# A linear-attention stage between two expert blocks on one core: float32 key sums, scanned value sums, a softmax centred by ScalarE's bias, a state masked by GpSimd, and a new order of the stages

## The chip, the cores and the metric

The kernel runs on one core of one Trainium2 chip. Its engines are called PE (TensorE, matrix products; PEld is its weight load), DVE (VectorE), ACT (ScalarE), POOL (GpSimd) and SP (SyncE, which issues DMAs here). The metric is device time in microseconds (us) from launch to end, the median of several runs. Matrix products write to PSUM, eight banks of 128 x 512 float32; all else lies in SBUF. POOL works on SBUF alone here.

## The reference

One sequence of T = 2048 tokens with 128 features goes through three residual blocks, each behind a layer norm: an expert feed-forward (one shared and eight routed experts, the best two per token), an attention with 64 slots per head, and the same feed-forward again. The attention, for each of four heads of 32 features:

```
wk = exp(clip(x @ sk_w1 @ sk_w2 + sk_b2)); zk = cumsum(wk, over time)
S = where(mask, q @ k.T, 0)
p = softmax(S @ wk * scale / zk)                  # over 64 slots
wv = exp(clip(x @ sv_w1 @ sv_w2 + sv_b2)); zv = cumsum(wv, over time)
A = where(mask, (p / zv) @ wv.T, 0)
o = A @ v;  o = rmsnorm(o) * gnorm_w * g * sigmoid(g);  out = o @ Wo
```

So two running sums over time are wanted (zk and zv, 256 columns each for the four heads), and their inverses, and two products with a causal mask.

## The kernel before

Tokens are cut into 16 chunks of 128 (chunk c, its parity p for double buffers, its place n in the loop). What lies before a chunk is kept in PSUM as a running state: `state_ps` holds K'wk (256 columns) and wv'v (128 columns), and only the blocks in which both sides belong to one head are wanted. `copy_state` on ACT copies just these blocks to `state`, in six instructions, into a tile whose other parts were set to zero once.

A chunk passes through four stages, one step of the loop each; in one step the engines work at four chunks, called front, mid, last and end. There are 19 steps: four written out, twelve in a hardware loop of two steps a turn, three to drain. Each engine has its own list of what it does in a step, in a fixed order (`attn_step`), and waits on semaphores; the order written there is the order in which it runs.

Before the change, front projects q, k (`project`) and the slot logits (`slot_logits`), applies the rotary embedding (DVE multiplies, `rope_multiply`; POOL adds, `rope_add`), splits q and k into float16 parts (`qk_high`, `qk_low`), turns them (`turn_qk`), and multiplies and masks S (`scores`, `mask_s`). It clips and exponentiates the slots (`clip_slots`, `slots_exponent`), 512 columns for keys and values together, and splits the result into three bf16 parts: `slots_high` on ACT, `slots_rest` on POOL, `slots_middle` on ACT, `slots_low` on POOL. Mid sums the parts over time with a triangle of ones, three products of 512 columns (`running_sums`), and later adds the rest of the chunk in the same way (`add_sums`), so that `sum_ps` carries the sum on. The sum is inverted by a logarithm, an exponential and one Newton step (`sums_log`, `sums_first_inverse`, then on DVE `sums_product` and `sums_inverse`). Mid also turns the value slots (`turn_v`, `copy_value_slots`), forms the logits from the state and the chunk, scales them, takes the smallest per head (`soft_min`), subtracts it (`soft_centre`), exponentiates (`soft_exp`), multiplies by the inverse value sum (`prob_scale`) and turns the product (`turn_p`, `copy_p`). Last forms A (`weights_a`, `mask_a`) and o (`outputs`), divides by the softmax sum (`norm_shares`), gates (`gate_o` on POOL), and prepares the root mean square (`o_square`, `norm_squares`, `norm_variance`; `root_o` on POOL raises to the power -1/2). End applies it (`norm_apply`), turns, projects (`turn_o`, `copy_o`, `out_proj`) and adds the result to x (`add_y`).

While the loop drains, the next block's layer norm begins. In the step of the last chunk's outputs, DVE takes the moments of the first twelve chunks (`early_moments`), after `mask_a` and before `norm_shares`. POOL takes two roots from them in `tokens(2, 0, 2)`, called ahead of its list for that step; DVE uses them in two calls of `centre` ahead of the next step. Lines named below by L and a number are those of the profile.

## Time and profile before

| what | value |
|---|---|
| median of 3 runs | 506.77 us (506.55 to 506.98) |
| the profiled execution's own time, and its span | 506.91 us, 504.9 us |
| busy: PE, DVE, ACT, POOL | 446.7, 433.5, 316.5, 166.0 us |
| mean granted TensorE clock | 0.97 of full |

A busy share is an average over stages, and PE's busy time counts matrix products whose ends are modelled. Start times are from the start of the span. The attention stage fills about 192 to 345 us.

### The profile page before, as it was taken

Reading aid. Unit: us, or ns where it says so; the run is one execution under the profiler, and the core shown is the slowest. Engines: PE = TensorE matmul, PEld = TensorE weight load, DVE = VectorE, ACT = ScalarE, POOL = GpSimd, SP = SyncE. Lnnn points to the kernel's source line nnn. Section 1 sums busy time; section 2 is a strip of 40 time slices with the busy share of each in tenths; the row PEclk is TensorE's granted clock in tenths of the full one; section 3 lists DMA queues with packets and bytes.
Section 4 is the critical chain, followed back from the end, with each engine's and each line's share of the span. In section 5 each row is a group of like instructions: output and inputs, shape, how many; then the busy total and the mean of one; then the engine's idle time right before and its main releaser. Section 6 shows DMA issues by size and latency. Waiting matters only on the chain.

```text
span 504.9 us, 12339 instructions
## 1 busy us (share of the span) xinstructions
PE 446.7 (88%) x3879; PEld 313.0 (62%) x3895; DVE 433.5 (86%) x1139; ACT 316.5 (63%) x683; POOL 166.0 (33%) x199
## 2 busy tenths in 40 slices
PE   0787899999999775999999999975899999999996
PEld 0444566666666463788888888764456666666664
DVE  3699999999999963799999999975899999999996
ACT  3544455555555476889898989845555555555553
POOL 2999990000000236466666666633000000000000
PEclk9999999999999987799999999995999999999999
DMA  6222000000000000000000000000000000000002
GB/s 214 87 70 81 1 1 0 0 0 0 0 0 1 1 2 0 2 0 1 1 1 0 0 0 0 0 1 1 1 1 2 0 0 0 0 0 0 0 0 83
DMA packets 6697, 6.98 MB, mean 14 GB/s; under 512 B 818, under 2 KB 5170, under 8 KB 6676
## 3 DMA queue, kind: packets, MB, share of 16 engines
q1 hardware_dynamic: 6532, 6.33, 4.2%
q10 hardware_dynamic: 144, 0.39, 0.2%
q8 instruction: 11, 0.18, 0.2%
q14 instruction: 10, 0.08, 0.1%
HBM read 5.67 MB, written 1.05 MB: 13 GB/s over the span
## 4 chain that ended last, share of the span: by engine, by line
PE 55%; DVE 20%; ACT 10%; issue 8%; POOL 4%; DMA 1%; DVEq 1%; POOLq 0%; ACTq 0%
PE bank L1131 16%; PE bank L1143 10%; PE bank L1145 10%; PE bank L1144 10%; DVE h L807 4%; DVE h_lo L813 2%; ACT gate_s L313 2%; ACT qk_t L382 2%; DVE x L796 2%; DVE stats L705 1%; DVE pz L937 1%; PE bank L1325 1%; POOL rstd L543 1%; ACT slot_b L362 1%; ACT h_hi L318 1%
## 5 line engine op out<-in xcount | busy, mean ns | idle before, releaser
L318 ACT ACTIVATE h_hi<-h 128x512 f16<-128x512 f32 x144 | 90.7, 630 | 133.0 <-DVE h L807 133.0
L807 DVE SCALAR_TENSOR_TENSOR h<-bank,gate_s 128x512 f32<-128x512 f32 x144 | 99.4, 690 | 25.5 <-ACT gate_s L313 19.7
L1131 PE MATMUL bank<-w_hi,h_hi 128*128 (+1 forms) x576 | 104.9, 219 | 15.1 <-DVE h_lo L813 10.4
L1143 PE MATMUL bank<-xt_hi,w_hi 128*128 128x512 f16 x288 | 110.6, 384 | 0.0
L1144 PE MATMUL bank<-xt_hi,w_lo 128*128 128x512 f16 x288 | 110.4, 383 | 0.0
L1145 PE MATMUL bank<-xt_lo,w_hi 128*128 128x512 f16 x288 | 110.2, 383 | 0.0
L1131 PE MATMUL bank<-w_hi,h_lo 128*128 (+1 forms) x576 | 104.4, 219 | 0.0
L1131 PE MATMUL bank<-w_lo,h_hi 128*128 (+1 forms) x576 | 104.4, 219 | 0.0
L813 DVE TENSOR_TENSOR h_lo<-h,h_hi 128x512 f16<-128x512 f32 x144 | 102.4, 711 | 0.1
L796 DVE SCALAR_TENSOR_TENSOR x<-bank,wts,x 128x128 f32<-128x128 f32 x288 | 86.5, 343 | 1.3 <-PE bank L1131 0.9
L313 ACT ACTIVATE gate_s<-bank 128x512 f32<-128x512 f32 x144 | 83.4, 579 | 0.0
L1131 PEld LDWEIGHTS bank<-w_hi,h_hi 128*128 128x128 f16 x576 | 56.1, 97 | 39.9 <-DVE h_lo L813 13.1
L1131 PEld LDWEIGHTS bank<-w_lo,h_hi 128*128 128x128 f16 x576 | 56.3, 98 | 12.0
L1131 PEld LDWEIGHTS bank<-w_hi,h_lo 128*128 128x128 f16 x576 | 56.3, 98 | 0.0
L1145 PEld LDWEIGHTS bank<-xt_lo,w_hi 128*128 (+1 forms) x288 | 28.5, 99 | 34.8 <-issue 1.7
L541 POOL TENSOR_SCALAR var_e<-mv 128x4 f32<-128x4 f32 x12 | 3.4, 283 | 114.1 <-issue 93.7
L1143 PEld LDWEIGHTS bank<-xt_hi,w_hi 128*128 (+1 forms) x288 | 28.4, 99 | 19.3 <-issue 1.3
L1144 PEld LDWEIGHTS bank<-xt_hi,w_lo 128*128 (+1 forms) x288 | 28.4, 99 | 18.1 <-issue 1.1
L1098 PE MATMUL bank<-cst,xn 128*128 128x128 f32 x48 | 11.5, 392 | 14.6 <-ACT xn L290 14.6
L290 ACT ACTIVATE xn<-x,shift,rstd 128x128 f32<-128x128 f32 x32 | 13.6, 483 | 14.1 <-DVE shift L716 13.8
L620 POOL TENSOR_TENSOR slot_r<-slots,slot_b 128x512 f32<-128x512 f32 x16 | 18.5, 1158 | 8.9 <-ACT slot_b L362 5.9
L625 POOL TENSOR_TENSOR slot_b<-slot_r,slot_b 128x512 bf16<-128x512 f32 x16 | 18.4, 1153 | 3.5 <-ACT slot_b L367 3.5
(160 smaller groups left out, 851.7 us busy)
## 6 DMA issues: line engine op xcount, KB each, us to landing
wf<-in_w_ffn SPq DMA_DIRECT2D x8, 384.0 KB, 3.1
...
```

Source lines behind the costliest of these rows:

```text
L290: i = act.activation(xn[:, g % 2, c, :], x[:, g * GT + c, :], ACT.Identity, bias=shift[:, g, c:c + 1], scale=rstd[:, g, c:c + 1])
L313: act.activation(gate_s[:, ih, :], gate_ps[ih][:, :], ACT.Silu, scale=1.0 / (XS * WS)).then_inc(silu_done, 1)
L318: act.activation(h_hi[:, g, ih, :], h32[:, ih, :], ACT.Copy).then_inc(hhi_done, 1)
L620: nc.gpsimd.tensor_tensor(slot_r[:, :], slots[:, p, :], slot_b1[:, p, :], ALU.subtract).then_inc(S["slots_rest"], 1)
L625: nc.gpsimd.tensor_tensor(slot_b3[:, p, :], slot_r[:, :], slot_b2[:, p, :], ALU.subtract).then_inc(S["slots_b3"], 1)
L796: i = nc.vector.scalar_tensor_tensor(x[:, t, :], down_ps[j][:, c % 2 * P:(c % 2 + 1) * P], wts[:, t, e:e + 1] if isinstance(e, int) else w ...
L807: nc.vector.scalar_tensor_tensor(h32[:, ih, :], up_ps[ih][:, :], HS / (XS * WS), gate_s[:, ih, :], ALU.mult, ALU.mult).then_inc(hmul_done, 1)
L813: nc.vector.tensor_tensor(h_lo[:, g, ih, :], h32[:, ih, :], h_hi[:, g, ih, :], ALU.subtract).then_inc(hlo_done, 1)
L1131: i = mm(dst, hp[:, g, ih, c * P:(c + 1) * P], wcols(wp, e, at, D), start=(k == 0), stop=(k == 3 * IH - 1))
L1143: mm(ps[:, :], wcols(w_hi, e, at, P), xt_hi[:, ts], start=True, stop=False)
L1144: mm(ps[:, :], wcols(w_lo, e, at, P), xt_hi[:, ts], start=False, stop=False)
L1145: mm(ps[:, :], wcols(w_hi, e, at, P), xt_lo[:, ts], start=False, stop=True).then_inc(done, 1)
```

## The change

The three bf16 parts are dropped. Key sums are one float32 product of 256 columns with the triangle (and one with its rest), straight from `slots`. Value sums are taken on DVE: `turn_v` moves to the front stage, where the slots lie turned with time along the columns, and `value_sums` runs a scan over the 128 columns of each half, which starts from the last column of the chunk before. The inverse is formed as before, in two halves where its input comes from two places. The softmax is no longer centred by DVE: `soft_exp` passes the smallest value as the bias of four instructions, one a head. The probabilities are turned without the inverse value sum, and `prob_scale`, now on the turned tile, multiplies by it out of PSUM. ACT copies the whole state in one instruction (`state_raw`), and POOL multiplies it by a tile of zeros and ones (`blocks`, `mask_state`). The tile of the projection and that of the turned p move to other PSUM banks. `turn_p`, `prob_total`, `prob_scale`, `prob_invert` move to the stage last, `norm_squares`, `norm_variance` and `root_o` to the stage end, `copy_state` and `copy_value_slots` to the front. All four orders are new, and POOL's `tokens(2, 0, 2)` stands one step later. The rest of the diff renames semaphores and declares tiles.

```diff
@@ -352,19 +350,8 @@
+        act.wait_ge(S["sums_added"], c - 1)
...
-def slots_high(c, p, n):
-    act.wait_ge(S["clip_done"], c + 1)
-    if n >= 2:
-        act.wait_ge(S["back_done"], c - 1)
-    act.activation(slot_b1[:, p, :], clipped[:, p, :], ACT.Exp, scale=1.0 / WS).then_inc(S["slots_b1"], 1)
-def slots_middle(c, p, n):
-    act.wait_ge(S["slots_rest"], c + 1)
-    act.activation(slot_b2[:, p, :], slot_r[:, :], ACT.Copy).then_inc(S["slots_b2"], 1)
@@ -391,7 +378,9 @@
-    act.activation(slot_ln[:, :], sum_ps[:, :], ACT.Ln).then_inc(S["sums_ln"], 1)
+    act.activation(slot_ln[:, 0:HM], ksum_ps, ACT.Ln)
+    act.wait_ge(S["v_summed"], c + 1)
+    act.activation(slot_ln[:, HM:2 * HM], v_sums[:, p, :, :].rearrange("p a t -> p (a t)"), ACT.Ln).then_inc(S["sums_ln"], 1)
 def sums_first_inverse(c, p, n):
@@ -413,32 +403,19 @@
         if n >= 2:
-            act.wait_ge(S["o_done"], c - 1)
-        for h in range(H):
-            rows, cols = slice(h * DK, (h + 1) * DK), slice(h * M, (h + 1) * M)
-            act.activation(state[rows, p, cols], state_ps[rows, cols], ACT.Copy)
-        for j in range(2):
-            rows = slice(j * M, (j + 1) * M)
-            i = act.activation(state[rows, p, HM:].rearrange("p (a b d) -> p a b d", a=2, d=DK)[:, :, j, :],
-                               state_ps[rows, HM:HM + 4 * DK].rearrange("p (a b d) -> p a b d", a=2, d=DK)[:, :, j, :],
-                               ACT.Copy)
-        i.then_inc(S["state_copied"], 1)
+            act.wait_ge(S["state_copied"], c - 1)
+        act.activation(state_raw[:, :], state_ps[:, 0:HM + 4 * DK], ACT.Copy).then_inc(S["raw_copied"], 1)
 def soft_exp(c, p, n):
-    act.wait_ge(S["centred"], c + 1)
-    if n >= 1:
-        act.wait_ge(S["pz_done"], c)
+    act.wait_ge(S["min_done"], c + 1)
+    if n >= 1:
+        act.wait_ge(S["p_turned"], c)
...
-    act.activation(prob[:, :], logit_c[:, :], ACT.Exp, scale=-DK ** -0.5).then_inc(S["prob_done"], 1)
-def copy_p(c, p, n):
-    act.wait_ge(S["pz_turned"], c + 1)
-    if n >= 2:
-        act.wait_ge(S["o_done"], c - 1)
-    act.activation(p_t[:, p, :, :], pz_t_ps.rearrange("p (a b) -> p a b", a=2), ACT.Copy, scale=-1.0).then_inc(S["p_copied"], 1)
+    for h in range(H):
+        hs = slice(h * M, (h + 1) * M)
+        i = act.activation(prob[:, hs], logit[:, hs], ACT.Exp, scale=-1.0, bias=logit_min[:, h:h + 1])
+    i.then_inc(S["prob_done"], 1)
 def o_square(c, p, n):
@@ -456,34 +433,28 @@
 def attn_step(i, n):
     front, mid, last, end = stages(i, n)
-    if mid:
-        copy_state(*mid)
     if mid:
         sums_log(*mid)
     if mid:
         sums_first_inverse(*mid)
     if front:
         qk_high(*front)
+    if front:
+        copy_state(*front)
+    if front:
+        slots_exponent(*front)
     if end:
         copy_o(*end)
     if front:
-        slots_high(*front)
-    if front:
-        slots_exponent(*front)
-    if mid:
-        copy_value_slots(*mid)
-    if front:
         copy_qk_parts(*front)
+    if front:
+        copy_value_slots(*front)
     if mid:
         soft_exp(*mid)
-    if front:
-        slots_middle(*front)
     if last:
         o_square(*last)
     if front:
         copy_q(*front)
-    if mid:
-        copy_p(*mid)
 def before(i):
@@ -604,25 +575,22 @@
-for zeros in (state[:, :, :], zero16[:, :], vslot_t[:, :, :, :, :]):
+for zeros in (state[:, :, :], zero16[:, :], vslot_t[:, :, :, :, :], v_sums[:, :, :, :]):
...
-nc.gpsimd.tensor_copy(tri16[:, :], tri)
-nc.gpsimd.tensor_copy(rest16[:, :], rest)
+nc.gpsimd.memset(blocks[:, :], 0.0).then_inc(S["blocks_set"], 1)
...
+nc.gpsimd.memset(ones32[:, :], 1.0)
...
-def slots_rest(c, p, n):
-    pool.wait_ge(S["slots_b1"], c + 1)
-    pool.wait_ge(S["slots_exp"], c + 1)
-    if n >= 1:
-        pool.wait_ge(S["slots_b3"], c)
-    nc.gpsimd.tensor_tensor(slot_r[:, :], slots[:, p, :], slot_b1[:, p, :], ALU.subtract).then_inc(S["slots_rest"], 1)
-def slots_low(c, p, n):
-    pool.wait_ge(S["slots_b2"], c + 1)
-    nc.gpsimd.tensor_tensor(slot_b3[:, p, :], slot_r[:, :], slot_b2[:, p, :], ALU.subtract).then_inc(S["slots_b3"], 1)
 def rope_add(c, p, n):
@@ -636,6 +604,14 @@
+def mask_state(c, p, n):
+    if n >= 1:
+        pool.wait_ge(S["raw_copied"], c)
+        if n >= 2:
+            pool.wait_ge(S["o_done"], c - 1)
+        nc.gpsimd.tensor_tensor(state[:, p, :], state_raw[:, :], blocks[:, :], ALU.mult).then_inc(S["state_copied"], 1)
 def qk_low(c, p, n):
@@ -654,20 +630,18 @@
     front, mid, last, end = stages(i, n)
     if front:
         rope_add(*front)
+    if end:
+        root_o(*end)
     if front:
         qk_low(*front)
     if front:
-        slots_rest(*front)
+        mask_state(*front)
     if last:
         gate_o(*last)
-    if front:
-        slots_low(*front)
-    if last:
-        root_o(*last)
 def before(i):
-    if i == NC + 1:
+    if i == NC + 2:
         tokens(2, 0, 2)
 tokens(1, 0, NG)
@@ -894,12 +868,26 @@
+def value_sums(c, p, n):
+    dve.wait_ge(S["vslot_turned"], c + 1)
+    if n >= 2:
+        dve.wait_ge(S["sums_prod"], c - 1)
+    if n >= 1:
+        dve.wait_ge(S["v_summed"], c)
+    for a in range(2):
+        i = nc.vector.tensor_tensor_scan(v_sums[:, p, a, :], ones32[:, :], vslot_t_ps[:, a * P:(a + 1) * P],
+                                         v_sums[:, 1 - p, a, P - 1:P], ALU.mult, ALU.add)
+    i.then_inc(S["v_summed"], 1)
 def sums_product(c, p, n):
...
-    nc.vector.tensor_tensor(slot_zi[:, :], sum_ps[:, :], slot_i0[:, :], ALU.mult).then_inc(S["sums_prod"], 1)
+    nc.vector.tensor_tensor(slot_zi[:, 0:HM], ksum_ps, slot_i0[:, 0:HM], ALU.mult)
+    nc.vector.tensor_tensor(slot_zi[:, HM:2 * HM], v_sums[:, p, :, :].rearrange("p a t -> p (a t)"), slot_i0[:, HM:2 * HM],
+                            ALU.mult).then_inc(S["sums_prod"], 1)
 def sums_inverse(c, p, n):
@@ -920,21 +910,14 @@
-def soft_centre(c, p, n):
-    lv = logit[:, :].rearrange("p (h m) -> p h m", h=H)
-    dve.wait_ge(S["min_done"], c + 1)
-    if n >= 1:
-        dve.wait_ge(S["prob_done"], c)
-    nc.vector.tensor_tensor(logit_c[:, :].rearrange("p (h m) -> p h m", h=H), lv,
-                            logit_min[:, :].unsqueeze(2).broadcast_to([P, H, M]), ALU.subtract).then_inc(S["centred"], 1)
 def prob_scale(c, p, n):
-    dve.wait_ge(S["prob_done"], c + 1)
-    if n >= 1:
-        dve.wait_ge(S["pz_turned"], c)
-    nc.vector.tensor_tensor(pz[:, :], prob[:, :], slot_inv[:, p, HM:2 * HM], ALU.mult).then_inc(S["pz_done"], 1)
+    dve.wait_ge(S["p_turned"], c + 1)
+    dve.wait_ge(S["sums_inv"], c + 1)
+    if n >= 2:
+        dve.wait_ge(S["o_done"], c - 1)
+    nc.vector.scalar_tensor_tensor(p_t[:, p, :, :].rearrange("p a t -> p (a t)"), p_t_ps, -1.0, slot_inv[:, p, HM:2 * HM],
+                                   ALU.mult, ALU.mult).then_inc(S["p_scaled"], 1)
 def prob_total(c, p, n):
@@ -1003,38 +986,38 @@
     front, mid, last, end = stages(i, n)
     if front:
         rope_multiply(*front)
+    if end:
+        norm_squares(*end)
+    if last:
+        prob_total(*last)
+    if last:
+        prob_scale(*last)
+    if end:
+        norm_variance(*end)
     if front:
         clip_slots(*front)
+    if last:
+        prob_invert(*last)
+    if mid:
+        sums_product(*mid)
     if end:
         norm_apply(*end)
+    if mid:
+        sums_inverse(*mid)
     if last:
         mask_a(*last)
     if last:
         early_moments(*last)
     if mid:
-        sums_product(*mid)
-    if mid:
-        sums_inverse(*mid)
-    if mid:
         soft_scale(*mid)
+    if front:
+        value_sums(*front)
+    if end:
+        add_y(*end)
     if mid:
         soft_min(*mid)
-    if mid:
-        soft_centre(*mid)
     if last:
         norm_shares(*last)
-    if mid:
-        prob_scale(*mid)
-    if mid:
-        prob_total(*mid)
-    if last:
-        norm_squares(*last)
-    if end:
-        add_y(*end)
-    if last:
-        norm_variance(*last)
-    if mid:
-        prob_invert(*mid)
     if front:
         mask_s(*front)
@@ -1205,10 +1188,11 @@
 def project(c, p, n):
     if n >= 1:
-        pe.wait_ge(S["qk_t_copied"], c)
+        pe.wait_ge(S["v_summed"], c)
+        pe.wait_ge(S["vslot_copied"], c)
...
-    three(qk_ps[:, 0:2 * D], (xt_hi[:, bass.ds(c * P, P)], xt_lo[:, bass.ds(c * P, P)]),
+    three(proj_ps, (xt_hi[:, bass.ds(c * P, P)], xt_lo[:, bass.ds(c * P, P)]),
...
 def slot_logits(c, p, n):
@@ -1247,20 +1233,17 @@
 def turn_v(c, p, n):
...
-    if n >= 1:
-        pe.wait_ge(S["p_copied"], c)
+    pe.wait_ge(S["rope_parts"], c + 1)
...
 def running_sums(c, p, n):
-    pe.wait_ge(S["slots_b3"], c + 1)
+    pe.wait_ge(S["slots_exp"], c + 1)
...
-    for k, part in enumerate((slot_b1, slot_b2, slot_b3)):
-        i = mm(sum_ps[:, :], tri16[:, :], part[:, p, :], start=(n == 0 and k == 0), stop=True, skip_group_check=True)
-    i.then_inc(S["sums_done"], 1)
+    mm(ksum_ps, tri, slots[:, p, 0:HM], start=(n == 0), stop=True, skip_group_check=True).then_inc(S["sums_done"], 1)
 def logits_of_earlier(c, p, n):
@@ -1281,13 +1264,12 @@
 def add_sums(c, p, n):
...
-    for part in (slot_b1, slot_b2, slot_b3):
-        mm(sum_ps[:, :], rest16[:, :], part[:, p, :], start=False, stop=True, skip_group_check=True)
+    mm(ksum_ps, rest, slots[:, p, 0:HM], start=False, stop=True, skip_group_check=True).then_inc(S["sums_added"], 1)
 def add_state(c, p, n):
     if n >= 1:
-        pe.wait_ge(S["state_copied"], c)
+        pe.wait_ge(S["raw_copied"], c)
@@ -1296,15 +1278,18 @@
 def turn_p(c, p, n):
-    pe.wait_ge(S["pz_done"], c + 1)
-    pe.wait_ge(S["vslot_copied"], c + 1)
+    pe.wait_ge(S["prob_done"], c + 1)
+    if n >= 1:
+        pe.wait_ge(S["p_scaled"], c)
+    if n >= 2:
+        pe.wait_ge(S["y_added"], c - 1)
...
-        i = nc.tensor.transpose(pz_t_ps[:, a * P:(a + 1) * P], pz[:, a * P:(a + 1) * P], ident)
-    i.then_inc(S["pz_turned"], 1)
+        i = nc.tensor.transpose(p_t_ps[:, a * P:(a + 1) * P], prob[:, a * P:(a + 1) * P], ident)
+    i.then_inc(S["p_turned"], 1)
 def weights_a(c, p, n):
-    pe.wait_ge(S["p_copied"], c + 1)
+    pe.wait_ge(S["p_scaled"], c + 1)
@@ -1341,32 +1328,32 @@
     front, mid, last, end = stages(i, n)
     if front:
         project(*front)
-    if front:
-        slot_logits(*front)
     if mid:
         running_sums(*mid)
     if last:
-        weights_a(*last)
+        turn_p(*last)
     if mid:
-        turn_v(*mid)
-    if end:
-        turn_o(*end)
+        add_state(*mid)
+    if front:
+        slot_logits(*front)
     if mid:
         logits_of_earlier(*mid)
     if mid:
         logits_of_chunk(*mid)
+    if last:
+        weights_a(*last)
+    if mid:
+        add_sums(*mid)
+    if end:
+        turn_o(*end)
+    if front:
+        turn_v(*front)
+    if front:
+        turn_qk(*front)
     if end:
         out_proj(*end)
-    if front:
-        turn_qk(*front)
     if last:
         outputs(*last)
-    if mid:
-        add_sums(*mid)
-    if mid:
-        add_state(*mid)
-    if mid:
-        turn_p(*mid)
     if front:
         scores(*front)
```

## Rows read from the trace of the kernel before

**Rows 1.** Busy time by stretch, the attention loop: engine, busy us, number of instructions, clock.

```profile
217.60:327.60 110.00, 104.00 (x845) 89.86 (x857) 103.00 (x250) 99.19 (x276) 70.78 (x93) 1.00 0.00 0
```

**Rows 2.** Timeline of DVE in the attention stage: start, length, instruction.

```profile
210.33 0.41 DVE L873 TENSOR_TENSOR rope_c<-bank,cst 128x256 f32<-128x256 f32 x1
...
226.94 0.41 DVE L873 TENSOR_TENSOR rope_c<-bank,cst 128x256 f32<-128x256 f32 x1
...
228.46 0.68 DVE L956 TENSOR_TENSOR a_masked<-bank,cst 128x512 f32<-128x512 f32 x1
229.06 0.68 DVE L902 TENSOR_TENSOR slot_zi<-bank,slot_i 128x512 f32<-128x512 f32 x1
229.77 1.13 DVE L907 SCALAR_TENSOR_TENSOR slot_inv<-slot_zi,slot_i 128x512 f32<-128x512 f32 x1
...
232.87 0.43 DVE L937 TENSOR_TENSOR pz<-prob,slot_inv 128x256 f32<-128x256 f32 x1
233.21 0.41 DVE L942 TENSOR_REDUCE prob_sum<-prob 128x4 f32<-128x256 f32 x1
...
233.99 0.76 DVE L985 TENSOR_SCALAR o_var<-o_ss 128x4 f32<-128x4 f32 x1
...
235.33 0.41 DVE L873 TENSOR_TENSOR rope_c<-bank,cst 128x256 f32<-128x256 f32 x1
...
238.46 0.69 DVE L907 SCALAR_TENSOR_TENSOR slot_inv<-slot_zi,slot_i 128x512 f32<-128x512 f32 x1
...
319.52 0.41 DVE L873 TENSOR_TENSOR rope_c<-bank,cst 128x256 f32<-128x256 f32 x1
...
334.42 0.15 DVE L985 TENSOR_SCALAR o_var<-o_ss 128x4 f32<-128x4 f32 x1
```

**Rows 3.** Timeline of POOL in one step of the attention loop.

```profile
229.69 0.67 POOL L643 TENSOR_TENSOR qk_parts<-qk,qk_parts 128x256 f16<-128x256 f32 x1 [0.83 <-ACT qk_parts L375]
...
233.57 1.15 POOL L625 TENSOR_TENSOR slot_b<-slot_r,slot_b 128x512 bf16<-128x512 f32 x1
234.83 1.02 POOL L570 TENSOR_TENSOR o_rstd<-o_var,power 128x4 f32<-128x4 f32 x1
```

**Rows 4.** Timeline of DVE in the first and the second feed-forward block.

```profile
41.17 1.01 DVE L813 TENSOR_TENSOR h_lo<-h,h_hi 128x512 f16<-128x512 f32 x1
42.10 1.11 DVE L782 TENSOR_TENSOR pick<-pick,share 128x128 f32<-128x128 f32 x2
...
371.25 0.49 DVE L782 TENSOR_TENSOR pick<-pick,share 128x128 f32<-128x128 f32 x2
```

**Rows 5.** Timeline of POOL in the first feed-forward block.

```profile
41.79 2.38 POOL L559 TENSOR_SCALAR wsc<-wf 128x768 f32<-128x768 f32 x1 [0.16 <-POOL w_lo L563]
```

**Rows 6.** Groups of ACT by line and shape, attention loop: busy us, mean ns, idle before.

```profile
L420 ACT ACTIVATE state<-bank 32x64 f32<-32x64 f32 x54 | 11.4, 212 | 0.5
...
L434 ACT ACTIVATE prob<-logit_c 128x256 f32<-128x256 f32 x13 | 5.4, 416 | 0.2 <-DVE logit_c L929 0.2
```

**Rows 7.** Timeline of PE in one step of the attention loop.

```profile
226.42 0.81 PE L1262 MATMUL bank<-slot_b,tri 128*128 128x512 bf16 x3
...
232.99 0.59 PE L1291 MATMUL bank<-slots,qk 128*128 128x256 f32 x2
```

**Rows 8.** Timeline of PE, the scores of the last chunk.

```profile
326.76 0.39 PE L1244 MATMUL bank<-qk_t 96*128 96x128 f16 x4
```

**Rows 9.** Timeline of DVE while the loop drains.

```profile
340.08 0.26 DVE L972 TENSOR_TENSOR o<-bank,prob_inv 128x128 f32<-128x128 f32 x1
...
344.53 0.29 DVE L1000 TENSOR_TENSOR x<-bank,x 128x128 f32<-128x128 f32 x1 [1.73 <-PE bank L1338]
```

**Rows 10.** Timeline of POOL while the loop drains.

```profile
337.91 0.23 POOL L541 TENSOR_SCALAR var_e<-mv 128x4 f32<-128x4 f32 x1 [2.25 <-DVE mv L709]
...
339.73 1.04 POOL L543 TENSOR_TENSOR rstd<-var_e,power 128x4 f32<-128x4 f32 x1
...
341.35 1.12 POOL L570 TENSOR_TENSOR o_rstd<-o_var,power 128x4 f32<-128x4 f32 x1 [0.16 <-DVE o_var L985]
```

More of the change, by code:

```diff
@@ L163, in macaron_kernel @@
         gates = sb("gates", [P, NC, D])
+        state_raw = sb("state_raw", [P, HM + 4 * DK])
+        blocks = sb("blocks", [P, HM + 4 * DK])
         state = sb("state", [P, 2, HM + 2 * 2 * DK])
@@ L171, in macaron_kernel @@
         logit_min = sb("logit_min", [P, H])
-        logit_c = sb("logit_c", [P, HM])
         prob = sb("prob", [P, HM])
@@ L203, in macaron_kernel @@
         q_t_ps = slots_ps[:, 0:P]
+        ksum_ps = sum_ps[:, 0:HM]
         qk_t_ps = qk_ps[:, :].bitcast(F16)
         logit_ps, o_ps = s_ps[:, 0:HM], c_ps[:, 0:P]
-        vslot_t_ps, pz_t_ps = vturn_ps[:, 0:HM], vturn_ps[:, HM:2 * HM]
-        o_t_ps, y_ps = oturn_ps[:, 0:P], oturn_ps[:, P:2 * P]
+        vslot_t_ps, proj_ps = vturn_ps[:, 0:HM], vturn_ps[:, HM:2 * HM]
+        o_t_ps, y_ps, p_t_ps = oturn_ps[:, 0:P], oturn_ps[:, P:2 * P], oturn_ps[:, HM:2 * HM]
         def stacked(q_block, k_block):
@@ L403, in copy_value_slots @@
                 act.wait_ge(S["vslot_turned"], c + 1)
+                act.wait_ge(S["v_summed"], c + 1)
                 if n >= 2:
@@ L606, in _ @@
             pool.wait_ge(ones_set, 1)
-            for zeros in (state[:, :, :], zero16[:, :], vslot_t[:, :, :, :, :]):
+            for zeros in (state[:, :, :], zero16[:, :], vslot_t[:, :, :, :, :], v_sums[:, :, :, :]):
                 nc.gpsimd.memset(zeros, 0.0)
-            nc.gpsimd.tensor_copy(tri16[:, :], tri)
-            nc.gpsimd.tensor_copy(rest16[:, :], rest)
+            nc.gpsimd.memset(blocks[:, :], 0.0).then_inc(S["blocks_set"], 1)
+            pool.wait_ge(S["blocks_set"], 1)
+            for h in range(H):
+                i = nc.gpsimd.memset(blocks[h * DK:(h + 1) * DK, h * M:(h + 1) * M], 1.0)
+            i.then_inc(S["blocks_set"], 1)
+            pool.wait_ge(S["blocks_set"], 2)
+            for j in range(2):
+                rows = slice(j * M, (j + 1) * M)
+                i = nc.gpsimd.memset(blocks[rows, HM:].rearrange("p (a b d) -> p a b d", a=2, d=DK)[:, :, j, :], 1.0)
+            i.then_inc(S["blocks_set"], 1)
+            pool.wait_ge(S["blocks_set"], 3)
+            nc.gpsimd.memset(ones32[:, :], 1.0)
             nc.gpsimd.tensor_copy(ident16[:, :], ident).then_inc(ones_set, 1)
             pool.wait_ge(ones_set, 2)
-            def slots_rest(c, p, n):
-                pool.wait_ge(S["slots_b1"], c + 1)
-                pool.wait_ge(S["slots_exp"], c + 1)
-                if n >= 1:
-                    pool.wait_ge(S["slots_b3"], c)
-                nc.gpsimd.tensor_tensor(slot_r[:, :], slots[:, p, :], slot_b1[:, p, :], ALU.subtract).then_inc(S["slots_rest"], 1)
-            def slots_low(c, p, n):
-                pool.wait_ge(S["slots_b2"], c + 1)
-                nc.gpsimd.tensor_tensor(slot_b3[:, p, :], slot_r[:, :], slot_b2[:, p, :], ALU.subtract).then_inc(S["slots_b3"], 1)
             def rope_add(c, p, n):
@@ L868, in rope_multiply @@
                 half = DK // 2
-                src = qk_ps[:, 0:2 * D].rearrange("p (a b j) -> p a b j", b=2, j=half)
+                src = proj_ps.rearrange("p (a b j) -> p a b j", b=2, j=half)
                 dst = rope_s[:, :].rearrange("p (a b j) -> p a b j", b=2, j=half)
@@ L873, in rope_multiply @@
                 nc.vector.tensor_tensor(rope_c[:, :].rearrange("p (a j) -> p a j", j=half),
-                                        qk_ps[:, 0:2 * D].rearrange("p (a j) -> p a j", j=half),
+                                        proj_ps.rearrange("p (a j) -> p a j", j=half),
                                         cos.unsqueeze(1).broadcast_to([P, 4 * H, half]), ALU.mult)
@@ L913, in soft_scale @@
                 dve.wait_ge(S["sums_inv"], c + 1)
-                nc.vector.tensor_tensor(logit[:, :], logit_ps, slot_inv[:, p, 0:HM], ALU.mult).then_inc(S["logit_scaled"], 1)
+                if n >= 1:
+                    dve.wait_ge(S["prob_done"], c)
+                nc.vector.scalar_tensor_tensor(logit[:, :], logit_ps, DK ** -0.5, slot_inv[:, p, 0:HM], ALU.mult,
+                                               ALU.mult).then_inc(S["logit_scaled"], 1)
             def soft_min(c, p, n):
@@ L1332, in turn_o @@
                     pe.wait_ge(S["y_added"], c)
+                if n + 1 < NC:
+                    pe.wait_ge(S["p_scaled"], c + 2)
                 nc.tensor.transpose(o_t_ps, o3[:, :], ident).then_inc(S["o_turned"], 1)
```

24 lines of the change are left out of this document (11 added, 13 removed).

## The prediction

> **What bounds the kernel now.** I read the busy time by stretch first. The kernel runs a feed-forward block, an attention stage and a second feed-forward block. The diff touches only the attention stage and the setup ahead of it, so the feed-forward blocks keep their time. Inside the attention loop three engines are nearly full at once [rows 1]: of 110.0 us PE is busy 104.00, DVE 103.00, ACT 99.19 and POOL 70.78. Next I read DVE's order of time. The third chunk's rope product starts at 210.33 and the sixteenth's at 319.52: 13 steps of 8.40 us [rows 2]. One step from 226.94 to 235.33 has 19 DVE instructions and hardly a gap, so DVE looks like the bound.
>
> But the 19 instructions do not need 8.39 us. Start to start, with nothing in the way, a 128x512 instruction takes 0.60 (the mask of A at 228.46 to the product at 229.06), a 128x256 one 0.34 (232.87 to 233.21), a 128x128 one, by an estimate from these two, about 0.20. Five of the first, six of the second, six of the third and two tiny ones come to 6.4 us. The other 2 us are waits. The two large ones [rows 2, 3] have a common cause. o_var, a 128x4 instruction, takes 0.76 at 233.99 but 0.15 at 334.42 with POOL idle [rows 2]; it ends within 0.03 us of the end of POOL's 1.15 us subtraction, which started at 233.57 [rows 3]. slot_inv takes 1.13 at 229.77 and 0.69 at 238.46 [rows 2]; in the first case POOL's 0.67 us subtraction for q and k ran from 229.69 to 230.36 [rows 3]. So a DVE instruction whose inputs all lie in SBUF waits out a POOL instruction.
>
> Who goes next when both queue? In the first feed-forward block h_lo held DVE from 41.17 to 42.18, POOL's tensor_scalar was issued meanwhile at 41.79, and the two picks that DVE had right behind h_lo, at 42.10, took 1.11 us [rows 4, 5]; the same two take 0.49 at 371.25, with POOL idle [rows 4]. POOL, having asked first, went between two adjacent DVE instructions. This is the row the forecast rests on. The Trainium skill, "SBUF — State Buffer", section "Who interferes with whom", says the same as a rule: a VectorE instruction with two SBUF inputs contends with a GpSimd instruction that reads SBUF, the pair of ports is an exclusive lock, and issue order decides who blocks. By that rule the change is exposed where VectorE does SBUF work beside the new mask on GpSimd, and the trace agrees, with 0.44 and 0.61 us lost to it in a step; with it the sum is my forecast's, without it the first rival's.
>
> **The change, part by part, in a step of the loop.**
>
> PE: each of the two sums was three bf16 products of 512 columns, 0.81 us for three records [rows 7]; each becomes one float32 product of 256 columns, and that is 0.59 for its two records, as the key state's product has it [rows 7]. That saves 0.22 twice. PE's busy 104.00 of 110.0 is 7.94 in a step of 8.40, so 7.5 remain. One wait comes on top: turn_p now stands third in PE's order and waits for prob, the last long work of ACT's step before, with add_state, slot_logits and everything else queued behind it. I put it at 0.3. PE's floor is 7.8.
>
> ACT: two 128x512 passes, six state copies of 0.21 [rows 6] and the copy of p go; one 128x512 copy comes. The logarithm is split in two. soft_exp becomes four instructions of 64 columns with a pointer bias: between 4 x 0.21, as the 32x64 copies [rows 6], and 4 x 0.42, as the 256-column exponential [rows 6]. I take 1.0 against 0.42, near the lower end, since the width is that of the copies. ACT loses about 1.5 us of its 7.6 in a step and is not the bound.
>
> POOL: two 128x512 subtractions of 1.15 [rows 3] go, one 128x512 mask comes, so 1.15 too.
>
> DVE: the centring goes (0.34). The product is cut into two halves (+0.06). Two scans of 128 columns come. No row shows a scan: the lower bound is a plain 128-column instruction from PSUM, 0.20, the upper a 128x512 one, 0.60. I take 0.34 each, the 256-column row between them. The Trainium skill, "DVE: opcode table, instruction layouts, handler registers and perf-mode slots", section "Datapath and trigger behaviour", has the built-in scan at half throughput; by that it would be the 256-column price too, and no run here shows it yet. DVE without waits: 6.4 - 0.34 + 0.06 + 0.68 = 6.8.
>
> Now the waits. After the rope product DVE does two reductions, prob_scale and o_var; root_o on POOL follows o_var and takes 1.02 [rows 3]. So root_o ends about when DVE is in the second half of the product, which reads SBUF alone. POOL's next is qk_low (0.67): its input from ACT is ready by then, by some 0.3 us. norm_apply needs root_o's result, so it always asks after qk_low: it waits about 0.5. Behind qk_low mask_state is ready (ACT's copy of the state is done 0.6 us earlier) and POOL goes from one instruction to the next without a gap, so it asks while norm_apply runs. By the pick rows it goes next, and sums_inverse waits about 1.05. With 0.1 at o_var, where POOL's rope sums end, and 0.1 for outputs, which now wait for the mask of A behind it: 6.8 + 0.5 + 1.05 + 0.2 = 8.55. Thirteen steps: 13 x (8.55 - 8.40) = +2.0.
>
> The first two steps: the chain of the three parts through POOL (1.15 twice [rows 3]) is gone from ahead of the first sums, but turn_v, the value copy and add_state now stand ahead of the next projection and clip. I take +0.4, between -1 and +1.5.
>
> The end costs most. Before, the scores of the last chunk start at 326.76 [rows 8] and its output is added at 344.53 [rows 9], 17.8 us later. POOL's two roots for the next norm (337.91 to about 340.8 [rows 10]) ran under DVE's moments, and the last chunk's root_o followed at 341.35 [rows 10]. After, root_o of the chunk before must come first, so the two roots stand after gate_o of the last chunk, which waits for norm_shares (340.08 [rows 9]), behind all moments. Two roots at 1.5 are 2.9 us in the open; DVE's two centrings and the last norm_squares wait for them, and root_o is behind both: +3.5. Further ahead, the last softmax waits for add_y of an earlier chunk and for 0.6 more of exponential, and the mask of A waits for norm_apply, whose root now comes a step later: +1.4 after the copy of p and the centring are taken off. Together +4.9, between +3.5 and +6. The setup's extra memsets on POOL run long before the attention stage, in its idle time: nothing, or their few tenths each if that cover were gone.
>
> Sum: 2.0 + 0.4 + 4.9 = +7.3, on the profiled run's 506.91: 514.2. That run lies 0.14 above the median of 506.77, so I say **514**.
>
> **The rivals.** First: sums_inverse gets in before mask_state, because DVE's next instruction asks earlier than its row shows or because ACT's copy of the state is late. The step then falls to PE's floor of 7.8: 13 x -0.6 = -7.8, with +0.4 and +4.9, and -0.3 for the last, shorter step: -2.8, 504. For it: PE and ACT really lose work. Against: the picks. It decides from a step under 8.0, where 13 steps win back the 5.3 of both ends. Second: only qk_low meets DVE, because qk_hi is a few tenths late (the margin is 0.3), and mask_state goes after sums_inverse. 8.55 less the mask's 1.05, plus PE's waits, is about 8.1: -3.9 + 5.3 = +1.4, 508.3. Third: a dear scan at 0.60 each adds 0.52 to a full DVE: 13 x 0.67 + 5.3 = +14, 521. That the edits do not do what they say I exclude: they change named instructions.
>
> **How the numbers follow.** My forecast 0.48, passing first 0.20, only qk_low 0.24, dear scan 0.08. About 0.2% (1.0 us) is what a measurement of this kernel tells from no change. Faster by more: 0.17 of the first rival and 0.02 of the second, 0.19. Within: 0.03 and 0.06, 0.09. Slower: 0.72. The range 504 to 519.5 leaves out the dear scan and the lower half of the first rival. The forecast's own range, from the bounds of the ends and a tenth either way in the step, is 511 to 517.
>
> **What would show it.** In the loop: sums_inverse at 1.6 to 1.8 us with POOL's mask beside it, and a step near 8.55 between rope products. A sums_inverse at 0.69 and steps of 7.8 would show the first rival. At the end: POOL's two roots after gate_o of the last chunk, and 22 to 23 us from the last scores to the last add. PE's sums at 0.59 each, scans at 0.4. If the end costs nothing, or the scans cost 0.2, the forecast is too high.

## The result, and the profile after

The changed kernel takes 510.78 us (median of 20 runs), the kernel before 508.01 (20 runs beside them; the three runs named above gave 506.77): a ratio of **1.0049, interval 1.0036 to 1.0062**, some 2.5 us slower. The forecast was 514, or +7.3: the sign is right, the size is not. The three places of the sum, from the two profiled executions (start to start on DVE and PE):

| stretch | before | after | difference | forecast |
|---|---|---|---|---|
| start to first rope product | 192.94 | 194.23 | +1.3 | 0 |
| first to fourth rope product (fill) | 25.61 | 28.22 | +2.6 | +0.4 |
| fourth to sixteenth (12 steps) | 100.97 | 95.99 | -5.0 | |
| sixteenth to the scores of chunk 15 | 7.24 | 6.63 | -0.6 | +2.0 with the line above |
| those scores to the last add (drain) | 17.77 | 23.07 | +5.3 | +4.9 |
| last add to end | 160.37 | 160.76 | +0.4 | 0 |

The first line is not the change's: the first feed-forward block is untouched, and in the other kernels of this study it ends between 192.85 and 195.09. The attention stage gives +2.3, where the medians differ by 2.8. The forecast drew its border elsewhere: its fill is the first two steps alone (17.39 before, 18.69 after, +1.3), and the third step (8.22 before, 9.53 after, +1.3) counts among its thirteen of the loop.

Busy time by stretch, after: the three steps of the fill and the loop. Columns: stretch, its length, busy us (instructions) of PE, PEld, DVE, ACT and POOL, granted clock (1.00 is 2.4 GHz), DMA share and GB/s.

```profile
194.23:202.66 8.43, 3.46 (x20) 2.69 (x20) 2.96 (x8) 4.35 (x8) 3.17 (x7) 0.63 0.00 0
202.66:212.92 10.26, 8.60 (x38) 7.07 (x38) 5.71 (x13) 5.62 (x14) 2.50 (x4) 0.50 0.00 0
212.92:222.45 9.53, 8.94 (x59) 7.73 (x58) 6.74 (x17) 5.74 (x15) 2.95 (x5) 0.79 0.01 3
222.45:318.40 95.95, 92.39 (x770) 82.66 (x768) 91.66 (x252) 75.27 (x206) 48.70 (x71) 1.00 0.00 0
```

The same stretches of the kernel before, which [rows 1] don't reach:

```profile
192.94:200.87 7.93, 2.86 (x18) 1.96 (x17) 2.11 (x5) 4.62 (x8) 5.14 (x9) 0.63 0.00 0
200.87:210.33 9.46, 8.31 (x43) 6.33 (x44) 6.07 (x14) 6.34 (x16) 4.18 (x6) 0.59 0.00 0
210.33:218.55 8.22, 7.62 (x61) 6.35 (x61) 7.62 (x18) 7.80 (x23) 4.81 (x7) 1.00 0.01 3
```

A step of the loop went from 8.41 to 8.00 us, and PE is now busy 7.70 of it. The fill's steps are each longer, and in the second and third the granted clock is lower than before: 0.50 is 1.2 GHz, and 0.79 is a step that is only partly at 2.4. DVE in one step of the loop after, which answers to [rows 2], then POOL in the same step, which answers to [rows 3], and ACT's copy of the state:

```profile
254.58 0.42 DVE L847 TENSOR_TENSOR rope_c<-bank,cst 128x256 f32<-128x256 f32 x1 [0.17 <-PE bank L1165]
...
257.66 0.76 DVE L976 SCALAR_TENSOR_TENSOR o<-o,o_rstd 128x128 f32<-128x128 f32 x1
258.35 0.68 DVE L895 SCALAR_TENSOR_TENSOR slot_inv<-slot_zi,slot_i 128x512 f32<-128x512 f32 x1
...
259.88 0.84 DVE L879 TENSOR_TENSOR_SCAN v_sums<-ones,v_sums,bank 128x128 f32<-128x128 f32 x2
...
262.47 0.42 DVE L847 TENSOR_TENSOR rope_c<-bank,cst 128x256 f32<-128x256 f32 x1 [0.16 <-PE bank L1165]
```

```profile
257.44 0.83 POOL L619 TENSOR_TENSOR qk_parts<-qk,qk_parts 128x256 f16<-128x256 f32 x1
261.51 1.00 POOL L613 TENSOR_TENSOR state<-state_raw,blocks 128x384 f32<-128x384 f32 x1 [3.24 <-PE bank L1310]
```

```profile
257.02 0.47 ACT L407 ACTIVATE state_raw<-bank 128x384 f32<-128x384 f32 x1
```

norm_apply (L976) waits out qk_low, 0.76 us for an instruction that takes 0.29 in the drain: as forecast. sums_inverse (L895) takes 0.68 and meets nothing. POOL's mask of the state (L613) isn't right behind qk_low (L619): POOL idles 3.24 us first, until PE's outputs (L1310), though the copy that it reads is done at 257.49. The groups of the loop say the same of all twelve steps (columns: count, busy us, mean ns, idle before):

```profile
L417 ACT ACTIVATE prob<-logit,logit_min 128x64 f32<-128x64 f32 x50 | 13.3, 336 | 0.3
...
L613 POOL TENSOR_TENSOR state<-state_raw,blocks 128x384 f32<-128x384 f32 x12 | 12.0, 1001 | 39.2 <-PE bank L1310 39.2
...
L895 DVE SCALAR_TENSOR_TENSOR slot_inv<-slot_zi,slot_i 128x512 f32<-128x512 f32 x12 | 8.1, 679 | 0.0
```

The drain after, from the last scores on PE, then on DVE and on POOL, which answers to [rows 8, 9, 10]:

```profile
325.07 0.39 PE L1230 MATMUL bank<-qk_t 96*128 96x128 f16 x4
```

```profile
340.15 0.28 DVE L955 TENSOR_TENSOR o<-bank,prob_inv 128x128 f32<-128x128 f32 x1
342.32 0.16 DVE L690 SCALAR_TENSOR_TENSOR shift<-mv,rstd 128x4 f32<-128x4 f32 x1 [1.89 <-POOL rstd L514]
...
343.93 0.16 DVE L690 SCALAR_TENSOR_TENSOR shift<-mv,rstd 128x4 f32<-128x4 f32 x1 [0.93 <-POOL rstd L514]
...
346.12 0.29 DVE L976 SCALAR_TENSOR_TENSOR o<-o,o_rstd 128x128 f32<-128x128 f32 x1 [1.12 <-POOL o_rstd L541]
348.14 0.29 DVE L983 TENSOR_TENSOR x<-bank,x 128x128 f32<-128x128 f32 x1 [1.73 <-PE bank L1325]
```

```profile
340.51 0.46 POOL L627 TENSOR_TENSOR o<-o,gates 128x128 f32<-128x128 f32 x1 [4.91 <-DVE o L955]
...
341.25 1.04 POOL L514 TENSOR_TENSOR rstd<-var_e,power 128x4 f32<-128x4 f32 x1
...
342.86 1.04 POOL L514 TENSOR_TENSOR rstd<-var_e,power 128x4 f32<-128x4 f32 x1
345.08 1.01 POOL L541 TENSOR_TENSOR o_rstd<-o_var,power 128x4 f32<-128x4 f32 x1 [1.19 <-DVE o_var L968]
```

The two roots (L514) stand in the open behind gate_o(15) (L627), and DVE waits 1.89 and 0.93 us for them.

### The profile page after: what moved, and what is told of

It reads as the page before. It is cut to its first block, busy times and chain, and to the rows that moved or that the text cites. A ratio compares the mean times of both kernels' runs of the same rounds, so it can differ in the third digit from the quotient of the medians.

```text
span 508.9 us, 12261 instructions
## 1 busy us (share of the span) xinstructions
PE 450.8 (89%) x3863; PEld 319.6 (63%) x3863; DVE 429.0 (84%) x1171; ACT 296.5 (58%) x624; POOL 145.3 (29%) x189
## 3 DMA queue, kind: packets, MB, share of 16 engines
HBM read 5.67 MB, written 1.05 MB: 13 GB/s over the span
## 4 chain that ended last, share of the span: by engine, by line
PE 72%; DVE 13%; issue 6%; ACT 5%; POOL 2%; DMA 1%; DVEq 0%; POOLq 0%; ACTq 0%
PE bank L1114 16%; PE bank L1126 10%; PE bank L1127 10%; PE bank L1128 10%; DVE h L781 4%; PE bank L1298 3%; PE bank L1261 2%; DVE h_lo L787 2%; PE bank L1310 2%; ACT gate_s L311 2%; PE bank L1219 2%; PE bank L1267 2%; PE bank L1273 2%; DVE x L770 1%; PE bank L1254 1%
## 5 line engine op out<-in xcount | busy, mean ns | idle before, releaser
L1114 PE MATMUL bank<-w_hi,h_hi 128*128 (+1 forms) x576 | 106.5, 221 | 13.3 <-DVE h_lo L787 8.6
L1114 PE MATMUL bank<-w_hi,h_lo 128*128 (+1 forms) x576 | 106.0, 221 | 0.0
L1114 PE MATMUL bank<-w_lo,h_hi 128*128 (+1 forms) x576 | 106.0, 221 | 0.0
L787 DVE TENSOR_TENSOR h_lo<-h,h_hi 128x512 f16<-128x512 f32 x144 | 100.7, 699 | 0.1
L613 POOL TENSOR_TENSOR state<-state_raw,blocks 128x384 f32<-128x384 f32 x15 | 15.0, 1000 | 47.0 <-PE bank L1310 47.0
L369 ACT ACTIVATE qk_t<-bank 96x1024 f16<-96x1024 f16 x16 | 16.3, 1019 | 13.7 <-PE bank L1219 13.7
```

What stands on the lines that cost most here:

```text
L369: act.activation(qk_t[0:STACK, p, :, :], qk_t_ps[0:STACK, :].rearrange("p (a t) -> p a t", a=2 * H), ACT.Copy).then_inc(S["qk_t_copied"], 1)
L613: nc.gpsimd.tensor_tensor(state[:, p, :], state_raw[:, :], blocks[:, :], ALU.mult).then_inc(S["state_copied"], 1)
L787: nc.vector.tensor_tensor(h_lo[:, g, ih, :], h32[:, ih, :], h_hi[:, g, ih, :], ALU.subtract).then_inc(hlo_done, 1)
L1114: i = mm(dst, hp[:, g, ih, c * P:(c + 1) * P], wcols(wp, e, at, D), start=(k == 0), stop=(k == 3 * IH - 1))
```

## The experiments

All are made from the changed kernel but the one that says otherwise. Line numbers in their rows can lie a few off.

**POOL's two roots earlier.** Theory: the drain's loss is the roots' place. The diffs here are shortened.

```diff
 (POOL, attn_step)
+if n == NC + 1:
+    tokens(2, 0, 2)
 if last:
     gate_o(*last)
-def before(i):
-    if i == NC + 2:
-        tokens(2, 0, 2)
```

> The changed kernel with one move: POOL's two roots for the next norm stand in the step of the last chunk's outputs, between root_o of the chunk before and gate_o, so under DVE's moments. Theory (the drain's loss is these two roots in the open): from the last scores to the last add 20 us in place of 23.1, the kernel 2.8 to 3.2 us faster than the changed one, so within 0.2% of the kernel before. Rival (the loss is the later softmax and the root that comes a step later): the last add moves by under 1 us, and the ratio to before stays near 1.005.

Ratio to the kernel before 0.9977 (0.9957 to 0.9996), median 507.24: 3.5 us below the change. The drain went from 23.07 to 20.23 us; fill (28.16) and loop (95.98) stayed within 0.1. The first feed-forward block, which the edit doesn't touch, ended 1.3 us earlier in this profile, so the 2.8 us of the drain are the safer price. That gives back just over half of the drain's 5.3; 2.5 remain. The roots now run under DVE's moments, and gate_o(15) follows them. POOL:

```profile
336.73 1.04 POOL L514 TENSOR_TENSOR rstd<-var_e,power 128x4 f32<-128x4 f32 x1
...
338.24 1.04 POOL L514 TENSOR_TENSOR rstd<-var_e,power 128x4 f32<-128x4 f32 x1
339.25 0.45 POOL L627 TENSOR_TENSOR o<-o,gates 128x128 f32<-128x128 f32 x1
```

**The mask of the state, held and unheld.** Would mask_state have met sums_inverse if it had been ready? Four buffers for the state, with the wait kept (the control), and with a wait that four buffers make needless.

```diff
-state = sb("state", [P, 2, HM + 2 * 2 * DK])
+state = sb("state", [P, 4, HM + 2 * 2 * DK])     # and state[:, n % 4, ...], loop unrolled by 4
 (the second kernel alone, in mask_state)
-if n >= 2:
-    pool.wait_ge(S["o_done"], c - 1)
+if n >= 4:
+    pool.wait_ge(S["o_done"], c - 3)
```

> The changed kernel with four state buffers and a hardware loop of four steps a turn, POOL's mask still waiting for the outputs of the same step: the control for the next run. Both theories: steps of 8.0 us as in the changed kernel, sums_inverse at 0.68, the time within 0.3% of the changed kernel.

> As the control, but with four buffers the mask waits only for the outputs of two steps earlier, so POOL can run it straight after qk_low. Theory A (the forecast's arbitration was right and only the mask's wait for the outputs kept it away): sums_inverse waits out the mask and takes 1.5 to 1.7 us, the step grows from 8.0 to 8.5 or more, the kernel is 5 to 9 us slower than the control. Theory B (DVE's next instruction goes first, or PE alone sets the step): sums_inverse stays near 0.7, the step within 0.1 us of the control, the time within 1.5 us of it.

The control: 1.0036 (1.0017 to 1.0055), 510.02 us, a step of 7.96, sums_inverse at 0.68. Unheld: **1.0242** (1.0211 to 1.0274), 521.17 us, 11.1 more than the control, a step of 8.81 on average. POOL and DVE of the unheld kernel:

```profile
260.55 0.83 POOL L619 TENSOR_TENSOR qk_parts<-qk,qk_parts 128x256 f16<-128x256 f32 x1
261.34 1.05 POOL L613 TENSOR_TENSOR state<-state_raw,blocks 128x384 f32<-128x384 f32 x1
```

```profile
260.77 0.76 DVE L976 SCALAR_TENSOR_TENSOR o<-o,o_rstd 128x128 f32<-128x128 f32 x1
261.45 1.49 DVE L895 SCALAR_TENSOR_TENSOR slot_inv<-slot_zi,slot_i 128x512 f32<-128x512 f32 x1
```

This is the picture that the forecast drew: mask_state right behind qk_low, asked for while norm_apply runs, ahead of sums_inverse, which takes 1.49 instead of 0.68. So it is in eleven of the twelve steps, which take 8.77 on average, 0.81 more than the control's 7.96: just what sums_inverse takes more. (In the twelfth PE is late, with a granted clock of 0.84; DVE comes after the mask, sums_inverse takes 0.68, the step 9.32.) The arbitration was forecast rightly; the wait of mask_state was not. The Trainium skill, "SBUF — State Buffer", section "Who interferes with whom", says that a VectorE instruction with two SBUF inputs contends with a GpSimd instruction that reads SBUF and that issue order decides. The control and this kernel agree, 0.68 against 1.49.

**project behind running_sums on PE.** Most of PE's idle time in the loop stands ahead of project, which waits for ACT's copy of the value slots.

```diff
-if front:
-    project(*front)
 if mid:
     running_sums(*mid)
+if front:
+    project(*front)
```

> The changed kernel with PE's project moved behind running_sums. Theory (PE's chain sets the loop, and its 0.2 us wait for the value copy ahead of project is on it): the wait goes, the step falls from 8.0 to about 7.8, 2 to 3 us off the changed kernel. Rival (DVE sets the step; its 0.16 us wait for project then grows by the 0.4 us that project is later): the step grows to 8.1 to 8.3, 1 to 4 us slower than the changed kernel.

1.0014 (0.9993 to 1.0036), 509.51 us; a step of 8.02 us, so the loop gained nothing. The wait only moved on: project has none, turn_p next behind it waits 0.30 to 0.51 us for ACT's prob. The rival's longer step didn't come either. The median lies 1.3 us below the change's, but the two intervals meet at 1.0036, so that is no clear gain.

**slot_logits behind project again.** In the fill clip_slots waits 1.99 and 1.60 us for slot_logits, which the change put behind add_state.

```diff
 if front:
     project(*front)
+if front:
+    slot_logits(*front)
 ...
 if mid:
     add_state(*mid)
-if front:
-    slot_logits(*front)
```

> TensorE's order alone is changed: slot_logits(c) stands right behind project(c), as it did in the kernel before, ahead of running_sums, turn_p and add_state. Theory A (the fill's loss is an order that makes clip_slots late): the two waits of clip_slots in steps 1 and 2 (1.99 and 1.60 us) fall below 0.3, the stretch from the first rope_multiply to the fourth falls from 28.2 to 26.2 to 27.2, and the time falls by 1 to 2 us. Theory B (the fill's loss is the granted clock, 0.50 in step 1, whatever the order): the waits fall, but the stretch stays at 27.8 to 28.5, since the same matmuls at 1.2 GHz fill the steps. Both: the loop's step stays at 7.9 to 8.1 us.

1.0431 (1.0409 to 1.0453), 529.94 us. In the fill clip_slots waits no more, and yet the stretch stayed (28.56, with 0.65, 0.50 and 0.76 granted): that speaks for theory B. The loop, where both expected no change, went to 9.53 a step. PE, then ACT, in the loop:

```profile
262.71 0.38 PE L1206 MATMUL bank<-wslots_st,low_st 98*128 98x512 f16 x1 [1.10 <-ACT q_t L374]
271.69 0.59 PE L1206 MATMUL bank<-wslots_st,low_st 98*128 98x512 f16 x1 [1.08 <-ACT q_t L374]
```

```profile
260.88 1.06 ACT L417 ACTIVATE prob<-logit,logit_min 128x64 f32<-128x64 f32 x4
261.85 0.29 ACT L425 ACTIVATE o_sq<-o 128x128 f32<-128x128 f32 x1
262.17 0.28 ACT L374 ACTIVATE q_t<-bank 128x128 f32<-128x128 f32 x1
```

slot_logits writes the bank in which the turned q of the chunk before still lies, and ACT copies that q last in its step, behind the four exponentials. Right behind project, the whole of PE's queue waits 1.1 us a step for it. That makes eight of the twelve steps 9.0 us. The other four take 10.6: in them the granted clock is 0.84, and the matmul behind the wait takes 0.59 instead of 0.38. One step of each kind, with the columns as above:

```profile
261.77:270.77 9.00, 7.70 (x64) 6.94 (x64) 7.67 (x21) 6.30 (x18) 4.13 (x7) 1.00 0.00 0
270.77:281.35 10.58, 9.29 (x64) 8.15 (x64) 7.68 (x22) 6.40 (x18) 3.98 (x7) 0.84 0.00 0
```

So a wait on PE can cost twice in the loop too: itself, and the clock behind it. With slot_logits in the place that the change gave it, the loop's step is 8.00.

**TensorE kept busy in step 0.** The other theory of the fill: the granted clock.

```diff
+def fill_pe(times):
+    for _ in range(times):
+        mm(state_ps[:, 0:HM + 4 * DK], zero16[:, 0:P], zero16[:, :], start=True, stop=True, skip_group_check=True)
 (PE, attn_step)
+if n == 0:
+    fill_pe(20)
 if front:
     turn_v(*front)
 if front:
     turn_qk(*front)
+if n == 0:
+    fill_pe(6)
```

> Work that changes nothing is put into TensorE's idle time of step 0: the matmul that clears the state's bank is issued 20 more times behind slot_logits(0) and 6 more times behind turn_qk(0) (26 x 0.16 us at 2.4 GHz, where TensorE idles 3.73 and 1.11 us). Theory B (the fill's loss is the clock that TensorE is granted after that idle time): the granted clock of steps 1 and 2 rises from 0.50 and 0.79 to above 0.9, the stretch from the first rope_multiply to the fourth falls from 28.2 to 24.5 to 26.5, and the time by 2 to 4 us. Theory A (an order that makes clip_slots late): the clock rises, but the stretch falls by under 1 us, because the waits for clip_slots and the copies stay. If the clock stays low all the same, the extra matmuls only add: 28.2 to 32 us.

**0.9952** (0.9932 to 0.9971), 505.50 us, 5.3 below the change. The fill went from 28.22 to 22.05 us, more than expected; loop (95.98) and drain (23.09) stayed. PE in step 0, of the changed kernel first, then of this one, and this one's steps of the fill:

```profile
198.14 0.69 PE L1238 MATMUL bank<-cst,slots 128*128 128x128 f32 x2 [3.73 <-ACT slots L354]
```

```profile
193.30 3.41 PE L1330 MATMUL bank<-zero 128*128 128x384 f16 x20
197.19 0.44 PE L1238 MATMUL bank<-cst,slots 128*128 128x128 f32 x2 [0.48 <-ACT slots L354]
```

```profile
193.28:200.65 7.37, 6.40 (x47) 3.96 (x46) 2.96 (x8) 4.34 (x8) 3.17 (x7) 1.00 0.00 0
200.65:207.57 6.92, 4.85 (x39) 3.85 (x37) 5.40 (x12) 5.31 (x13) 2.96 (x4) 1.00 0.01 2
207.57:215.33 7.76, 7.09 (x59) 6.18 (x57) 6.72 (x17) 5.74 (x16) 2.96 (x5) 1.00 0.00 1
```

The extra matmuls compute nothing. They take the place of 3.73 us of idle time, after which the clock had fallen to 1.2 GHz (the same two records take 0.69 there, 0.44 here), and the clock stays at 2.4 through all three steps. The waits of clip_slots shrink with it, from 1.99 and 1.60 to 0.58 and 0.44, in an order that is unchanged: the late slot_logits was for the most part the clock.

**The same in the kernel before** (20 ahead of turn_qk(0), 6 behind it). Does the loss belong to the change?

> The kernel before with the same 26 clearing matmuls in its own step 0 (20 ahead of turn_qk(0), 6 behind it). If the low clock of the first steps is a matter of TensorE's idle time in step 0 and not of the change, the kernel before gains too: its granted clock was 0.63 and 0.59 there and its first three steps took 25.61 us, so 23.0 to 24.5 us and a ratio of 0.994 to 0.998. If the change's own order makes the clock fall, the kernel before gains nothing (0.999 to 1.001).

0.9979 (0.9960 to 0.9998), 506.70 us; its fill went from 25.61 to 24.33. Its granted clock was 1.00 in the first and third steps, but still 0.81 in the second:

```profile
199.93:209.06 9.13, 6.65 (x42) 5.39 (x43) 6.06 (x15) 6.65 (x17) 4.51 (x6) 0.81 0.00 0
```

So the kernel before paid for its idle time too (3.96 us ahead of turn_qk(0)), 1.3 us at least, less than the change's 6.2. With the extra matmuls the changed fill, 22.05, is shorter than the old one with them (24.33) or without (25.61): what the change lost there is the clock. How much shorter the new order alone makes it is not shown, since no run holds the old one at 2.4 GHz throughout.

**Edits together.** First roots, slot_logits and extra matmuls; then roots and extra matmuls alone.

> Three edits together on the changed kernel: POOL's two roots ahead of gate_o(15), slot_logits behind project, and the 26 clearing matmuls in step 0. If the drain's loss (3 us, measured alone), the order and the clock are separate causes, their gains add: 3 + 1 to 2 + 2 to 4 us, the ratio to the kernel before 0.986 to 0.993. If the order and the clock are one cause (both only bring the fill's PE work forward), 0.993 to 0.996. If neither moves the fill, 0.997 to 0.998, as with the roots alone.

> The changed kernel with two edits that each gave time alone: POOL's two roots ahead of gate_o(15) (its profiled drain went from 23.07 to 20.23 us) and the 26 clearing matmuls in TensorE's idle time of step 0 (the fill went from 28.22 to 22.05 us). If the two places are independent, as the theory has it, the profile shows both (22.05 and 20.2), and the ratio to the kernel before comes to 0.986 to 0.991. If one of them is given back later, it is 0.993 to 0.997.

The three: 1.0371 (1.0330 to 1.0412), 525.89 us, fill 22.90, step 9.53, drain 20.21; the order of slot_logits costs the loop as much as alone (four steps of 10.6 again, at 0.84), which none of the three branches had in it. The two: **0.9875** (0.9857 to 0.9893), 501.30 us, fill 22.04, step 8.00, drain 20.24. The two gains add, and this version is faster than both kernels.

**The drain's clock and its moments.** From the last outputs on, the granted clock of the two-edit kernel is 0.50. Further extra matmuls in PE's idle time there (4 ahead of weights_a(15), 3 behind outputs(14), 20 behind outputs(15)), and then also DVE's third early moments behind norm_shares(15).

```diff
 (the second kernel alone, DVE)
-    for g in range(NG - 1):          # early_moments
+    for g in range(NG - 2):
 if last:
     norm_shares(*last)
+if n == NC + 1:
+    moments(2, NG - 2)
```

> The kernel with both edits, and further clearing matmuls in TensorE's idle time of the drain: 4 ahead of weights_a(15), 3 behind outputs(14), 20 behind outputs(15), where the granted clock was 0.50 from outputs(15) to the start of the second feed-forward part. If the clock follows TensorE's idle time there as in step 0, outputs(15) falls from 2.6 to 1.4 to 1.7 us, the turns ahead of the routing from 1.9 to 1.0, and the time by 1.5 to 3 us against the kernel with the two edits. If the drain is a chain of the other engines (POOL's roots, VectorE, ScalarE) in which TensorE has little part, it falls by under 0.7 us.

> The kernel with the clearing matmuls in step 0 and in the drain, and one more edit: of VectorE's three early moments ahead of norm_shares(15), the third (1.2 us) goes behind it. With the clock kept up in the drain, outputs(15) ended at 333.03 and norm_shares(15) came only at 334.92, behind the moments. If the moments are what swallowed the gain of the faster outputs, norm_shares(15) starts 1.0 to 1.6 us nearer to outputs(15)'s end and the stretch from the last scores to the last add falls from 19.79 to 18.3 to 19.0 us. If another wait stands behind (POOL's roots, ScalarE), it stays at 19.5 to 20. The time against the kernel before: 0.985 to 0.988, or 0.988 to 0.991.

First: 0.9905 (0.9876 to 0.9934), 502.79 us, drain 19.79 instead of 20.24, with 1.00 granted in it instead of 0.76. Second: 0.9894 (0.9862 to 0.9925), 502.78, drain 19.79 again. Neither time can be told from the two-edit kernel's. In the first, norm_shares(15) still came behind the third moments. In the second, norm_shares(15) came before the third moments, but gate_o(15) on POOL still waits for the second root. DVE, then POOL:

```profile
331.71 0.28 DVE L952 TENSOR_TENSOR o<-bank,prob_inv 128x128 f32<-128x128 f32 x1
```

```profile
332.36 1.17 POOL L514 TENSOR_TENSOR rstd<-var_e,power 128x4 f32<-128x4 f32 x1
333.37 0.45 POOL L627 TENSOR_TENSOR o<-o,gates 128x128 f32<-128x128 f32 x1
```

So the full clock is worth 0.45 us of the profile's drain, and a faster PE and an earlier DVE then both end at POOL's second root. That the rest of the drain hangs on POOL's order is read from these rows; no run moves the roots once more.

## Why the prediction was right or wrong

**The step that failed** is "Behind qk_low mask_state is ready". The copy of the state was ready; the buffer was not. With two buffers, mask_state's wait for o_done names the outputs of the last stage in the same step, and those come late in PE's list. The wait stands in the diff; the forecast asked only for the data. So mask_state runs 3.2 us after qk_low, beside DVE work that it doesn't delay, and sums_inverse keeps 0.68. That takes the 1.05 out of DVE's sum, which leaves 7.5; the step measured 8.00, with PE busy 7.70 of it and DVE 7.64, DVE waiting a few tenths for PE, and PE for ACT. So the forecast's 8.55 was 0.55 too long (-5.6 us over the twelve steps and the last one, where +2.0 stood). The unheld kernel shows the forecast's picture at 8.8.

What that forecast rested on was thinner than it says. The pick rows by themselves don't show POOL going between two DVE instructions: by the profile POOL's instruction of 41.79 runs 2.38 us, to 44.17, and the picks were done at 43.21. It is the unheld kernel that shows it. The rule that a DVE instruction with all inputs in SBUF waits out POOL is too wide as well: o_ss, a reduction from SBUF, begins beside the very subtraction that o_var waits out (233.57 to 234.72), and takes 0.29 as always:

```profile
233.59 0.29 DVE L978 TENSOR_REDUCE o_ss<-o_sq 128x4 f32<-128x128 f32 x1
```

And of the two losses named as agreeing with the page on SBUF, only slot_inv's 0.44 is of an instruction with two SBUF inputs; o_var, with 0.61, has one. The mask and the copy of the state are 384 columns wide, not 512: the mask takes 1.00, not 1.15, and in the unheld kernel sums_inverse loses 0.81 to it, not 1.05.

The rest of the step held: norm_apply waits about 0.5 (0.76 against 0.29), the scan costs 0.38 (0.76 from the start of the two to the next instruction; 0.34 was taken), the exponential 1.06 for four (1.0), a key sum 0.60 for two records (0.59). The Trainium skill, "DVE: opcode table, instruction layouts, handler registers and perf-mode slots", section "Datapath and trigger behaviour", has the built-in scan at half throughput. The trace agrees: 0.38 a scan, start to start, against 0.20 for a plain 128-column instruction. The step is the second rival's picture, a DVE that meets qk_low alone (8.1, 508.3), though for another reason than a late qk_hi. The first rival's floor of 7.8 for PE (7.5 of work and a wait of 0.3) is near as well: PE is busy 7.70 in a step and idle 0.30.

**The fill was mis-sized**: +0.4 was taken, +2.6 came (+1.3 in the forecast's two steps, inside its bounds of -1 to +1.5, and +1.3 in the third). The order of work was costed, the granted clock of these steps was not. It was in the trace of before (0.63 and 0.59). The change has about the same idle time in step 0 (3.73 and 1.11 us, against 3.96 and 1.11) and more of it in step 1 (1.66 us of the step, against 1.15), and stays at 1.2 GHz for longer. Held at 2.4, its fill takes 22.05, less than either fill of the kernel before.

**The drain was right**, part by part: +4.9 forecast, +5.3 measured. Behind norm_shares(15) it is 7.99 where it was 4.45, the +3.5 of the forecast, of which the roots' move alone gave back 2.8. Ahead of it, it is 15.08 where it was 13.32, +1.8 for the forecast's +1.4.

**The sum**: 7.3, less 7.6 in the loop, more 2.2 in the fill and 0.4 in the drain, is 2.3. The measured 510.78 falls inside the range but just below the forecast's own range (511 to 517). That is luck in part: two errors of opposite sign made the total look nearer than its terms were.

What stays open: why the granted clock of the kernel before is back at 1.00 in its third step and that of the change only part of the way through it; the rows show the longer waits beside it, not the cause. What makes up the drain's 1.8 ahead of norm_shares(15) no run takes apart.
